# Output stage of an attention and expert kernel: tile by tile, with kept means and centred weights

## The reference

```python
h = transpose(x, (1, 0, 2)); t = h           # x: layernorm(x1); t has tokens of 32 rows each
probs = softmax(h @ Wg); idx = sort(top_k(transpose(probs), cap))   # 16 heads
# q, k, v of the gathered rows; att = q k^T * scale, softmax over the rows' axis; av = p v
ao = einsum('hbid,hde->hbie', av, Wo) + bo
outs = zeros_like(t).at[b_ids, tok].add(ao)
y = t + outs
mu = mean(y, axis=-1); var = var(y, axis=-1)
yn = (y - mu) * rsqrt(var + 1e-05) * ln_g + ln_b
x = x + transpose(yn, (1, 0, 2))             # x here is x1
```

## Time and profile before

| | us |
|---|---|
| median of 3 runs | 1844.03 |
| lowest, highest | 1843.45, 1845.11 |
| the profiled execution | 1843.14 |
| its span in the trace | 1841.3 |
| TensorE busy | 1571.0 (85%) |
| VectorE busy | 1414.6 (77%) |
| GpSimd busy | 1266.8 (69%) |
| ScalarE busy | 1210.4 (66%) |
| output stage, first instruction to end | 1417.8 to 1841.3 |

### The profile page before, as it was taken

How to read it: one execution, slowest core, us unless ns; L and a number is a source line. 1 busy time by engine, 2 the same in 40 slices (tenths; PEclk the granted TensorE clock), 3 DMA queues, 4 the chain that set the end, 5 groups by cost and what they waited for, 6 DMA issues and landing times. The chain is left out here.

```text
span 1841.3 us, 58322 instructions
## 1 busy us (share of the span) xinstructions
PE 1571.0 (85%) x21933; PEld 1273.1 (69%) x22061; DVE 1414.6 (77%) x3007; ACT 1210.4 (66%) x2950; POOL 1266.8 (69%) x1235
## 2 busy tenths in 40 slices
PE   4899999999999999999999996899997877777763
PEld 3777777777777777777777775799996544444431
DVE  2578788787787787787787777687755399999998
ACT  3677777777777777777777764233332887878873
POOL 1576776777777767767777776578872568687664
PEclk9999999999999999999999998899998998989987
DMA  6123222232222322323223111745653176767776
GB/s 214 54 88 105 88 97 97 88 105 88 96 97 88 104 89 90 103 88 101 92 88 106 48 37 64 272 133 158 198 148 78 28 183 146 190 167 181 187 184 160
DMA packets 82021, 217.72 MB, mean 118 GB/s; under 512 B 13136, under 2 KB 14544, under 8 KB 72784
## 3 DMA queue, kind: packets, MB, share of 16 engines
q1 hardware_dynamic: 71504, 180.42, 33.3%
q0 software_dynamic: 10240, 33.56, 6.1%
HBM read 146.82 MB, written 67.11 MB: 116 GB/s over the span
## 5 line engine op out<-in xcount | busy, mean ns | idle before, releaser
L316 POOL TENSOR_TENSOR rec_hn<-rec_hn,rec_out_w 128x512 f32<-128x512 f32 x128 | 199.7, 1560 | 180.1 <-DVE rec_hn L743 180.1
L294 POOL TENSOR_TENSOR rec_hrs<-rec_harg,rec_minus_half 128x8 f32<-128x8 f32 x128 | 253.8, 1983 | 10.0
L1316 POOL TENSOR_TENSOR out_x_half<-out_x_half,ln_b 128x512 f32<-128x512 f32 x128 | 170.9, 1365 | 98.0 <-DVE out_z_half L1496 96.8
L1435 PE MATMUL out_z_ps<-probs_all,out_hot 128*128 128x512 f32 x256 | 150.3, 671 | 98.5 <-ACT probs_all L1362 52.4
L540 ACT ACTIVATE rec_d<-rec_l_ps 128x512 f32<-128x512 f32 x256 | 150.4, 587 | 41.0 <-PE rec_l_ps L448 40.7
L1004 PE MATMUL exp_q_ps<-exp_wqkv,exp_rows_t 128*128 128x192 f32 x1024 | 177.2, 327 | 0.0
L709 DVE TENSOR_TENSOR rec_c<-rec_s_ps,rec_d 128x512 f32<-128x512 f32 x256 | 164.5, 684 | 14.6 <-PE rec_s_ps L424 14.6
L1060 ACT ACTIVATE exp_rows_t<-exp_t_ps 128x512 f32<-128x512 f32 x128 | 69.4, 594 | 151.3 <-PE exp_t_ps L992 120.1
L955 POOL DMA_INDIRECT exp_x_rows<-x_scratch,rowid x128 | 135.5, 1059 | 45.3 <-issue 25.9
L763 DVE TENSOR_TENSOR rec_x_ring<-rec_x_ring,rec_hn 128x512 f32<-128x512 f32 x128 | 88.6, 692 | 100.3 <-POOL rec_hn L316 99.9
L1004 PEld LDWEIGHTS exp_q_ps<-exp_wqkv,exp_rows_t 128*128 128x128 f32 x1024 | 165.4, 190 | 0.4 <-ACT exp_rows_t L1060 0.3
(11 more groups left out here) (210 smaller groups left out, 4494.7 us busy)
## 6 DMA issues: line engine op xcount, KB each, us to landing
rec_x_ring<-in_x SPq DMA_DIRECT2D x128, 256.0 KB, 2.7
rec_ctx_ring<-in_ctx SPq DMA_DIRECT2D x128, 256.0 KB, 2.9
x_scratch<-rec_x_ring SPq DMA_DIRECT2D x128, 256.0 KB, 2.0
out_x_half<-x_scratch SPq DMA_DIRECT2D x128, 256.0 KB, 5.1
out<-out_x_half SPq DMA_DIRECT2D x128, 256.0 KB, 4.0
exp_wqkv<-in_wqkv SPq DMA_DIRECT2D x4, 1536.0 KB, 7.4
exp_x_rows<-x_scratch,rowid POOLq DMA_INDIRECT x128
wo<-in_wo SPq DMA_DIRECT2D x1, 2048.0 KB
```

What stands on the lines that cost most here:

```text
L294: nc.gpsimd.tensor_tensor(hrs[:, G % 2], harg[:, G % 2], mhalf[:], ALU.pow).then_inc(hrs_done, 1)
L316: nc.gpsimd.tensor_tensor(h, h, w8[:], ALU.mult).then_inc(hw_done, 1)
L1316: nc.gpsimd.tensor_tensor(xt[H % XR][:, q, :], xt[H % XR][:, q, :], lb[:], ALU.add).then_inc(xb_done, 1)
L1435: nc.tensor.matmul(z_ps[T % 3][:], hot[T % 4][:], ao[T % 4], start=True, stop=True).then_inc(z_full, 1)
```

## The change

The row mean of y = x1 + scatter(ao) is not computed in the output stage any more. The mean of x1 comes from the first stage: `token_moments` writes mean and variance of all rows to a table `moments`, which is kept, and the wait for `y_ve` goes. `by_row` turns the means round as a fourth table, `centres`. The output weights `wo` are centred in the expert stage by ScalarE (eight sums at units 40 to 47, eight subtractions at units 48 to 55), and `bo` by one TensorE and two VectorE instructions, so that the scattered rows have mean zero.

The output stage then goes by tile: `add(T)` (z_ps + x1 - its mean), `scale(T - 3)`, `finish(T - 7)`, with eight buffers of one tile for z. ScalarE squares all four tiles of a half, one per step (`square`), and the sum of squares is the variance. GpSimd adds `ln_b` once per tile and makes the scales of a half one tile into the next. x1 has five buffers, the fifth in the space of v of chunk 0, and is loaded five ahead. `mark` stays as it is.

```diff
@@ recurrence_stage, expert_stage
         def token_moments(G):
             dve.wait_ge(x1_done, G + 1)
-            if G >= 2 * NC:
-                dve.wait_ge(y_ve, G // NC - 1)
...
-            vec.bn_aggr(yagg[:, G % (2 * NC), :], ystat[:, G % 2, :]).then_inc(y_var, 1)
+            vec.bn_aggr(moments[:, G // NC, G % NC, :], ystat[:, G % 2, :]).then_inc(y_var, 1)
...
+                by_row(3, lambda c: moments[:, :, c, 0]).then_inc(tables_full, 1)
+            if m == 52:
+                pe.wait_ge(out_in, 64)
+                nc.tensor.matmul(m_ps[1][:, 0:KC], mean[:], bo[:], start=True, stop=True).then_inc(bo_full, 1)
...
+            if 40 <= m < 40 + NE // 2:
+                act.wait_ge(out_in, 64)
+                act.wait_ge(wo_sum, m - 40)
+                nc.scalar.activation(unused[:], wo[:, m - 40, :], ACT.Copy, scale=-1.0 / z.E,
+                                     accum_out=wo_mean[:, m - 40:m - 39]).then_inc(wo_sum, 1)
+            if 48 <= m < 48 + NE // 2:
+                act.wait_ge(wo_sum, m - 47)
+                nc.scalar.activation(wo[:, m - 48, :], wo[:, m - 48, :], ACT.Identity, bias=wo_mean[:, m - 48:m - 47]
+                                     ).then_inc(wo_centred, 1)
...
+                vec.tensor_copy(centres[:], m_ps[0][:, 3 * P:4 * P]).then_inc(tables_done, 1)
+            if m == 54:
+                dve.wait_ge(bo_full, 1)
+                link(vec.tensor_reduce(bo_mean[:], m_ps[1][:, 0:KC], AX.X, ALU.add))
+                link(vec.tensor_scalar(bo[:], bo[:], bo_mean[:, 0:1], None, ALU.subtract))
@@ output_stage
-    XR, ZR, LEAD, ON_ACT = 4, 2, 18, 3
+    XR, ZR, LEAD, SCALE, FINISH = 5, 8, 18, 3, 7
...
+            if H + XR < HALVES:
+                load(H + XR)
...
+        for T in range(TILES + 3):
+            if T < TILES:
+                pool.wait_ge(z_read, T + 1)
+                x1 = xt[T // 4 % XR][:, T % 4, :]
+                nc.gpsimd.tensor_tensor(x1, x1, lb[:], ALU.add).then_inc(xb_done, 1)
+            H, q = divmod(T, 4)
+            if q == 1 and H:
+                pool.wait_ge(square_done, 4 * H)
+                nc.gpsimd.tensor_tensor(ve[H % 2][:], var[H % 3][:], epsv[:, 4 * H - 4:4 * H], ALU.add).then_inc(ve_done, 1)
+                pool.wait_ge(ve_done, H)
...
+                nc.gpsimd.tensor_tensor(rs[H % 3][:], ve[H % 2][:], mhalf[:], ALU.pow).then_inc(rs_done, 1)
+            if q == 2 and T < TILES:
...
+                    attend(c + 1, n)
...
+        def square(T):
+            H, q = divmod(T, 4)
+            act.wait_ge(z_read, T + 1)
+            act.wait_ge(square_done, T)
...
+            nc.scalar.activation(dump[:], zt[T % ZR][:], ACT.Square, scale=E ** -0.5,
+                                 accum_out=var[(H + 1) % 3][:, q:q + 1]).then_inc(square_done, 1)
...
+        def add(T):
...
+            if T >= ZR:
+                dve.wait_ge(out_done, T - ZR + 1)
+            dve.wait_ge(z_full, T + 1)
+            vec.scalar_tensor_tensor(zt[T % ZR][:], xt[H % XR][:, q, :], centres[:, T:T + 1], z_ps[T % 3][:],
+                                     ALU.subtract, ALU.add).then_inc(z_read, 1)
...
+        def scale(T):
+            dve.wait_ge(square_done, T + 1)
+            vec.tensor_tensor(zt[T % ZR][:], zt[T % ZR][:], lg[:], ALU.mult).then_inc(zg_done, 1)
...
+            dve.wait_ge(rs_done, H + 1)
+            dve.wait_ge(xb_done, T + 1)
+            dve.wait_ge(zg_done, T + 1)
+            vec.scalar_tensor_tensor(x1, zt[T % ZR][:], rs[(H + 1) % 3][:, q:q + 1], x1, ALU.mult, ALU.add
+                                     ).then_inc(out_done, 1)
...
+        for T in range(TILES + FINISH):
+            if T < TILES:
+                add(T)
+            if 0 <= T - SCALE < TILES:
+                scale(T - SCALE)
+            if T >= FINISH:
+                finish(T - FINISH)
```

More of the change, by code:

```diff
@@ L1013, in by_row @@
                     mm = nc.tensor.matmul(m_ps[0][32 * j:32 * j + 32, P * where + 32 * c:P * where + 32 * c + 32],
-                                          table[:, c].rearrange("p h i -> p (h i)") if where < 2 else table[:, c],
+                                          table(c),
                                           at[:, :, j], start=True, stop=True)
@@ L1275, in load @@
                 sp.wait_ge(o_st[r], 64 * (H // XR))
+            elif H == XR - 1:
+                sp.wait_ge(av_done, 4)
             for j in range(4):
                 sp.dma_start(xt[r][j * NB:(j + 1) * NB], x_view[H, j]).then_inc(x_in[r], 16)
-        for H in range(3):
+        for H in range(XR):
             load(H)
@@ L1312, in _ @@
             attend(1, n)
-        for H in range(HALVES):
-            for q in range(4):
-                pool.wait_ge(z_read, 4 * H + q + 1)
-                nc.gpsimd.tensor_tensor(xt[H % XR][:, q, :], xt[H % XR][:, q, :], lb[:], ALU.add).then_inc(xb_done, 1)
-            pool.wait_ge(agg_done, (4 - ON_ACT) * (H + 1))
-            pool.wait_ge(square_done, ON_ACT * (H + 1))
-            nc.gpsimd.tensor_tensor(ve[H % 2][:], agg[H % 2][:, :, 1], epsv[:, 4 * H:4 * H + 4], ALU.add).then_inc(ve_done, 1)
-            pool.wait_ge(ve_done, H + 1)
-            if H >= 2:
-                pool.wait_ge(out_done, 4 * (H - 1))
-            nc.gpsimd.tensor_tensor(rs[H % 2][:], ve[H % 2][:], mhalf[:], ALU.pow).then_inc(rs_done, 1)
-            c, n = divmod(H + 3, 8)
-            if H == 0:
-                attend(1, 2)
-            if n < 4 and c + 1 < NC:
-                attend(c + 1, n)
+        for T in range(TILES + 3):
[8 more added lines that the diff above has]
+                pool.wait_ge(ve_done, H)
+                if H > 3:
+                    pool.wait_ge(out_done, 4 * (H - 3))
+                nc.gpsimd.tensor_tensor(rs[H % 3][:], ve[H % 2][:], mhalf[:], ALU.pow).then_inc(rs_done, 1)
+            if q == 2 and T < TILES:
+                c, n = divmod(H + 3, 8)
+                if H == 0:
+                    attend(1, 2)
+                if n < 4 and c + 1 < NC:
+                    attend(c + 1, n)
     def projected(u):
@@ L1389, in _ @@
                 put_rows(T + 2)
+            if T > 0:
+                square(T - 1)
             if T >= 0 and T % 32 in (0, 4, 8, 12) and T // 32 + 1 < NC:
@@ L1476, in finish @@
-        def finish(H):
-            dve.wait_ge(rs_done, H + 1)
-            dve.wait_ge(xb_done, 4 * H + 4)
-            dve.wait_ge(zg_done, 4 * H + 4)
-            for q in range(4):
-                x1 = xt[H % XR][:, q, :]
-                vec.scalar_tensor_tensor(x1, zt[H % ZR][:, q, :], rs[H % 2][:, q:q + 1], x1, ALU.mult, ALU.add
-                                         ).then_inc(out_done, 1)
+        def add(T):
+            H, q = divmod(T, 4)
+            if q == 0:
+                dve.wait_ge(x_in[H % XR], 64 * (H // XR + 1))
+            if T >= ZR:
[3 more added lines that the diff above has]
+                                     ALU.subtract, ALU.add).then_inc(z_read, 1)
@@ L1485, in _ @@
         for n in range(4):
             attend(n)
-        for H in range(HALVES):
-            s = H % 2
-            dve.wait_ge(x_in[H % XR], 64 * (H // XR + 1))
-            if H >= ZR:
-                dve.wait_ge(out_done, 4 * (H - ZR + 1))
-            for q in range(4):
-                T = 4 * H + q
-                dve.wait_ge(z_full, T + 1)
-                if q < ON_ACT:
-                    vec.scalar_tensor_tensor(zt[H % ZR][:, q, :], z_ps[T % 3][:], 1.0, xt[H % XR][:, q, :], ALU.mult, ALU.add,
-                                             accum_out=sums[s][:, q:q + 1]).then_inc(z_read, 1)
-                else:
-                    vec.tensor_tensor(zt[H % ZR][:, q, :], z_ps[T % 3][:], xt[H % XR][:, q, :], ALU.add).then_inc(z_read, 1)
-            dve.wait_ge(z_read, 4 * H + ON_ACT)
-            if H >= 2:
-                dve.wait_ge(square_done, ON_ACT * (H - 1))
-            vec.tensor_scalar(offs[s][:], sums[s][:], E ** -1.5, None, ALU.mult).then_inc(mean_done, 1)
-            vec.tensor_scalar(agg[s][:, 0:ON_ACT, 0], sums[s][:], 1.0 / E, None, ALU.mult).then_inc(mean_link, 1)
-            for q in range(ON_ACT, 4):
-                dve.wait_ge(z_read, 4 * H + q + 1)
-                vec.bn_stats(stat[s][:, q, :], zt[H % ZR][:, q, :]).then_inc(stat_done, 1)
-            for q in range(ON_ACT, 4):
-                dve.wait_ge(stat_done, (4 - ON_ACT) * H + q - ON_ACT + 1)
-                vec.bn_aggr(agg[s][:, q, :], stat[s][:, q, :]).then_inc(agg_done, 1)
-            if H:
-                scale(H - 1)
-                finish(H - 1)
```

74 lines of the change are left out of this document (29 added, 45 removed).

## The result

| | before | changed |
|---|---|---|
| median of 4 runs, us | 1844.57 | 1859.24 |
| lowest, highest | 1843.45, 1846.38 | 1857.49, 1860.89 |
| ratio to before, 95% interval | | 1.0078, 1.0061 to 1.0096 |
| the profiled execution | 1843.14 | 1858.46 |
| its span | 1841.3 | 1856.6 |

The changed kernel is 0.8% slower. The forecast was 1859.3.

A forecast was written before the change was run, and what follows sets the result against it. VectorE was taken to pace the output stage's tile loop. Steps and attention sums 12.2, tail 2.3 and expert stage 0.8 gave +15.3; 1843.1 + 15.3 + 0.9 = 1859.3 us, range 1832 to 1872.

The forecast's parts named there:

- The turn: Output loop: GpSimd's `ln_b` add goes between `scale` and `finish`, once per tile, costing VectorE 1.02 us.
- rival A: Output loop: GpSimd gets no turn between `scale` and `finish`; ScalarE's 2.55 us bounds up to tile 109; 1781 us, chance 0.13.
- The step itself: Output loop, `add` to `add`: 3.13 us a tile instead of 3.04, including 0.10 between `finish` and next `add`.
- The attention sums: Ten sums inside the output loop: four such steps take 12.64 us instead of 12.52, 1.2 us in all.
- The first step with a `finish`: Output loop's first tiles: no `finish` until tile 7, start left at 1463.10, then every step 3.13 us.
- The stores at the end: Stores behind the output loop's tail: claimed to be the same as before, 0 us.
- The tail of 18.9 us: Output loop from the start of tile 124: 18.9 us against 16.6 before, +2.3.
- the 27.2 us: Output stage before the change: given as VectorE's own idle time, nearly all before the first tiles.
- B: Output loop: power delays the `ln_b` add past its turn once per four tiles, `finish` goes first; 1835 us, chance 0.15.
- the door: Output loop: `ln_b` add gets ahead of `finish` if it starts before 1.27 us of the step; 1.06 expected behind the power.
- C: Output stage: TensorE's clock falls and TensorE becomes the bound; about 1873 us, chance 0.05.
- E: Output loop: GpSimd's power holds VectorE for its whole length, 13 us more; 1872 us, chance 0.03.

The follow-up runs named there:

- Experiments 1 to 5: GpSimd's `ln_b` add removed from the changed kernel (1776.84 us) and the kernel before (1803.91), or, in the changed kernel, halved (1797.25), delayed until `finish` (1832.55) or `scale` (1814.61).
- a_by_half_hot: Changed kernel with VectorE's order by half of four tiles, and the one-hot made by one GpSimd instruction instead of two on ScalarE: 1879.22 us.
- a_by_half: Changed kernel with VectorE doing four `add`, then four `scale` and four `finish` of the half before: 1815.53 us.
- a_pow_twice: Changed kernel with a second 128x4 power on GpSimd behind the first, into a spare tile: 1853.76 us.
- experiment 7: The run of a_pow_twice: changed kernel with the 128x4 power issued twice on GpSimd, 1853.76 us.

## Why the prediction was right, step by step

**The turn, right.** It stood on two spacings of one place of the trace of before, 1.13 and 0.55 us. Both hold in the changed kernel (1605.38 to 1606.51 to 1607.06), and the median `finish` of the stage is the 1.76 of this place. Experiments 1 to 5 show that it is this and no other thing: without the add 82 us go, with half of it the turn halves, and the same add a little later in the step costs 0.3 instead of 1.02.

**That rival A does not happen, right; its price, nearly.** GpSimd's add starts 0.83 after `add`, as foreseen, and has its turn. With the cause away the time was 1776.84, case A said 1781. That the two are so close is in part luck: ScalarE's steps, whose square takes 0.63 to the next start and not 0.72, made tile 7 to tile 109 6.6 us shorter than A had it, the last 15 steps were 2.08 and not 2.3, 3.3 us less, and against that this run reached tile 7 5.9 us later (1468.99).

**The step itself, 0.055 us too long.** The forecast was 3.13 in each tile. Measured are 3.06 three times and 3.12 once, 3.075 on the mean. The term that was mis-sized is the 0.10 between `finish` and the next `add`. It is 0.03 (1604.00 to 1604.03) in three tiles of four and 0.09 (1607.06 to 1607.15) at the first tile of a half. The row that I took it from, 1475.41, was just such a first tile, whose `add` has one wait more, that for the load of x1. A small number that is multiplied by 117 wants more than one row.

**The attention sums, too short.** A half with them takes 2.98 + 3.30 + 3.35 + 3.06 = 12.69 us. The prediction had 12.64, as 0.12 above its own quiet half of 12.52; the measured quiet half is 12.30, so each costs 0.39. Two of the ten fall before tile 7; the eight behind it cost 3.2 us where the prediction had 1.2 for all ten.

**The first step with a `finish`, missed.** I left the first tiles as they were. But GpSimd is still busy with `ln_b` adds then, and the first `finish` waits 2.44 us for its first power:

```profile
1463.64 0.75 DVE L1496 SCALAR_TENSOR_TENSOR out_z<-out_x_half,x_means,out_z_ps 128x512 f32<-128x512 f32 x1 [0.86 <-PE out_z_ps L1456]
1464.31 1.38 DVE L1501 TENSOR_TENSOR out_z<-out_z,ln_g 128x512 f32<-128x512 f32 x1
1468.13 1.77 DVE L1509 SCALAR_TENSOR_TENSOR out_x_half<-out_z,out_rs,out_x_half 128x512 f32<-128x512 f32 x1 [2.44 <-POOL out_rs L1344]
```

Tile 7 to tile 8 takes 6.35 us, 3.3 more than a step.

**The stores at the end, missed.** I said that they stay the same. The last two halves are now finished 2.7 us apart instead of 5.5. In both kernels their eight stores are issued in one row; the first line is the kernel before, the second the changed one:

```profile
1829.42 8.23 SPq L1284 DMA_DIRECT2D out<-out_x_half  x8
1846.21 6.84 SPq L1303 DMA_DIRECT2D out<-out_x_half  x8
```

Before, the last store was issued by 1837.65, 2.7 us behind the last `finish` (1834.92); now it is 1853.05, 4.2 behind it (1848.83). From the last `finish` to the end of the span it is 7.8 us where it was 6.4.

Against the two spans, which differ by 15.3 us, the terms are:

| | predicted | measured |
|---|---|---|
| up to tile 7 | +0.8 | +0.5 (1463.10 to 1463.64) |
| tile 7 to tile 124 | +12.2 | +11.4 (355.19 to 366.57 us) |
| tile 124 to the last `finish` | +2.3 | +2.0 (16.6 to 18.6 us) |
| last `finish` to the end | 0 | +1.4 |
| sum | +15.3 | +15.3 |

The hit to a tenth of a microsecond is luck in this: 117 x 0.055 = 6.4 us too much in the steps was made up by 2.0 us in the attention sums, 3.3 in the first gap, 0.3 in the step of tile 8 and 1.4 in the stores; 0.3 less up to tile 7 and 0.3 less in the tail balance the rest. The first row of the table is luck by itself: the changed kernel and its variants have the same two stages ahead, and yet their first `add` (a_by_half_hot left aside) starts anywhere from 1447.3 us, in the changed kernel, to 1453.2, in a_by_half. The mechanism and its size are not luck.

**Two workings that do not come out as written.** The tail of 18.9 us names three steps (9.4), three `scale` with `finish` (3.8) and four `finish` (2.6), 15.9 together; the other 3.0, called the pipeline's end, are about one more step, that of tile 127. And the 27.2 us of the earlier trace rows are the waits of L1496 for TensorE alone, not VectorE's idle time: between tile 7 and tile 124 VectorE was busy 335.14 of 355.19 us, so 20 us were idle, 7 of them in waits of L1499 for TensorE and 4 in waits of L1496 for loads of x1. In the changed kernel it is busy 358.30 of 366.57. That the loop runs at VectorE's pace holds, but 0.17 us of the 3.04 were waits.

**B, close, and its mechanism real.** The `ln_b` add behind the power starts 1.09 us after `add` (1602.06 to 1600.97), predicted 1.06, so the door stays open as forecast. a_pow_twice pushed it past and the kernel became faster. B's size was too large, though: it had the step behind the short one at 3.31, and it is 3.72, because the late add meets `scale` as well as its own successor.

**C and E, wrong, as weighted.** The granted clock of the stage is 0.99 against 0.92 before; the steps are even, and the longest wait of a scatter for VectorE is 1.8 us, against 3.8 before, so C did not come. E fell in experiment 7. The prediction cited the Trainium skill ("SBUF — State Buffer", section "SBUF: two separate sides") for a lock of the port pair over the full instruction. For full-width adds that agrees with the rows, where a turn costs VectorE 1.02 us; for the 128x4 power the measurement decides against it, since `scale` and `finish` beside two of them took 0.69 and 0.75. The small instructions do wait, though, when a `finish` runs: the variance add takes 0.65 beside one and 0.20 alone (at 1466.78).

**The start of the stage, only half settled.** The output stage starts 1.3 us later than before. But the point at which the tables are made was already 1.5 us later; the fourth table itself is about half a microsecond. I did not run the fourth table alone, so where the rest comes from stays open; it is well within the 6 us by which the first `add` moves between kernels with the same two stages ahead.
